# Mixer of a decoder layer, level 7: order of gate projection, output projection, gates, residual and moments

## The reference

```python
z = tanh((x + delta * mu_x) @ W_x1.T)             # delta: shifted x minus x
mus = einsum(z, W_x2) + x_bias                    # five of them: r, w, k, v, g
r, k, v, g = ((x + delta * mu) @ W.T ...)         # w: tanh(... @ A_w.T) @ B_w.T + b_w
def step(S, inp):
    kv = k_t[..., :, None] * v_t[..., None, :]
    o_t = einsum('bhk,bhkv->bhv', q_t, S + u * kv)
    return exp(w_t)[..., None] * S + kv, o_t
o = (o - mean) / sqrt(var + EPS)                  # per head
o = (o * gn_weight + gn_bias) * silu(g)
return o @ W_o.T
```

## Time and profile before

| | |
|---|---|
| median of the runs | 1555.5 us |
| profiled execution | 1543.22 us, span 1541.4 us |
| mean granted TensorE clock | 0.954 |
| PE busy | 1337.4 us, 87% of the span |
| PE weight loads (PEld) | 898.5 us, 58% |
| DVE busy | 992.6 us, 64% |
| POOL busy | 798.2 us, 52% |
| ACT busy | 576.4 us, 37% |

### The profile page before, as it was taken

The page is one execution under the profiler, slowest core; times in us unless marked ns, Lnnn a source line. Parts: engine busy times, 40 slices in busy tenths (PEclk is TensorE's granted clock), DMA queues, the critical chain, the costliest instruction groups (busy, mean ns, idle before and its releaser), DMA issues. The chain is left out here.

```text
span 1541.4 us, 31333 instructions
## 1 busy us (share of the span) xinstructions
PE 1337.4 (87%) x9914; PEld 898.5 (58%) x9915; DVE 992.6 (64%) x2041; ACT 576.4 (37%) x1420; POOL 798.2 (52%) x1138
## 2 busy tenths in 40 slices
PE   4787788778863899999999999999983999999996
PEld 2465455456552566666666666666652566666664
DVE  2687977977872378888888888888882222222221
ACT  1334233233320355555555555555541221212221
POOL 3235623633533567777777777777763222222222
PEclk9999999999976699999999999999995999999999
DMA  4995000000001554545455555555431223222231
GB/s 144 278 294 155 0 1 1 0 0 0 1 1 33 96 101 105 126 121 125 120 126 122 126 123 122 126 124 124 118 84 42 45 43 46 44 44 45 43 48 21
DMA packets 152681, 127.99 MB, mean 83 GB/s; under 512 B 41363, under 2 KB 145443, under 8 KB 152547
## 3 DMA queue, kind: packets, MB, share of 16 engines
q1 hardware_dynamic: 140242, 112.22, 29.7%
q0 software_dynamic: 12304, 14.10, 6.0%
HBM read 36.10 MB, written 44.83 MB: 53 GB/s over the span
## 5 line engine op out<-in xcount | busy, mean ns | idle before, releaser
L1365 DVE TENSOR_REDUCE neg_raw<-bank_s 100x2 f32<-100x722 f32 x256 | 229.0, 895 | 22.9 <-PE bank_s L1558 22.7
L1899 POOL DMA_INDIRECT out<-result,target x57 | 88.2, 1547 | 267.1 <-DVE result L1873 264.0
L1239 ACT ACTIVATE prob<-bank_st 120x400 f32<-120x400 f32 (+1 forms) x384 | 166.2, 514 | 152.2 <-PE bank_st L1577 152.2
L1376 DVE TENSOR_SCALAR bank_st<-bank_st 121x1200 f32<-121x1200 f32 x128 | 180.4, 1409 | 1.4 <-PE bank_st L1568 0.6
L751 PE MATMUL bank_l<-q_heads,k 128*100 128x192 f32 (+4 forms) x512 | 124.1, 383 | 63.9 <-DVE attn L565 51.0
L1884 DVE TENSOR_TENSOR hidden<-silu,ebank_v 128x512 f32<-128x512 f32 x57 | 39.2, 687 | 197.0 <-PE ebank_v L1808 197.0
L751 PEld LDWEIGHTS bank_l<-q_heads,k 128*100 128x100 f32 x512 | 81.4, 177 | 114.0 <-DVE attn L565 43.5
L399 ACT ACTIVATE q_heads<-q 32x192 f32<-32x192 f32 (+3 forms) x168 | 62.1, 369 | 226.1 <-DVE q L524 217.7
L1094 POOL TENSOR_TENSOR neg_diag<-xident_b,neg_max 100x400 bf16<-100x400 bf16 x128 | 109.1, 853 | 35.2 <-DVE neg_max L1370 34.6
L1558 PE MATMUL bank_s<-k_st,q_st 96*128 96x361 bf16 x512 | 123.2, 322 | 3.8 <-DVE neg_raw L1365 2.4
L1568 PE MATMUL bank_st<-q_st,k_st 96*128 96x100 bf16 x1536 | 112.8, 209 | 5.7 <-ACT prob L1239 0.6
(11 more groups left out here) (207 smaller groups left out, 2737.8 us busy)
## 6 DMA issues: line engine op xcount, KB each, us to landing
k_st<-k_part SPq DMA_DIRECT2D x384, 90.2 KB
slot_rows<-empty SPq DMA_DIRECT2D x9, 2967.0 KB, 28.8
q_st<-q_part SPq DMA_DIRECT2D x192, 50.0 KB
kv<-in_ctx_t SPq DMA_DIRECT2D x32, 270.8 KB
expert_w<-in_w SPq DMA_DIRECT2D x16, 512.0 KB, 4.4
rows<-slot_rows SPq DMA_DIRECT2D x57, 129.0 KB, 2.0
residual<-in_w SPq DMA_DIRECT2D x16, 256.0 KB, 4.3
residual<-in_x SPq DMA_DIRECT2D x8, 400.0 KB
```

What stands on the lines that cost most here:

```text
L1239: act.activation(prob[0:KEYS[c], t % 2, c], bank_st[0:KEYS[c], c, 0:4 * T], ACT.Exp).then_inc(exp_done, 1)
L1365: dve.tensor_reduce(neg_raw[:, h:h + 2], bank_s[0:T, :, 0:S], AX.X, ALU.max, negate=True).then_inc(max_done, 1)
L1376: dve.tensor_scalar(tile, tile, CLAMP, -CLAMP, ALU.min, ALU.max).then_inc(clipped, 1)
```

## The change

Nothing is computed otherwise. Four things change their place in the engines' programs.

- DVE: `norm_stats(g + 2)` goes from the begin of level 5 to level 7, behind the copies of that level. `front(g + 1, ..., 7)`, the two gates, goes ahead of `residual(g - 1)`, and `norm_apply(g + 2)` behind both.
- PE: in level 7 the gate projection (`front(g + 1, 7)`) goes ahead of `project_out(g - 1)`.
- POOL: `norm(g + 2)` goes behind `mix(g + 1, 4)`.
- ACT and SP keep their programs.

```diff
--- before.py
+++ after.py
@@ -315,10 +315,10 @@
                     mix(g + 1, 3)
                 if not first:
                     finish(g - 1, 1 - p, 3)
+                if more:
+                    mix(g + 1, 4)
                 if two_more(g):
                     norm(g + 2)
-                if more:
-                    mix(g + 1, 4)
             every_group(pool, body)
             head_norm(GROUPS - 1)
             for j in range(G):
@@ -611,8 +611,6 @@
                 for s in range(LEVELS):
                     if s == 0 and more:
                         front(g + 1, 1 - p, 1)
-                    if s == 5 and two_more(g):
-                        norm_stats(g + 2)
                     if s + 1 < LEVELS:
                         if s >= 1:
                             decay_q(g, p, s + 1)
@@ -630,11 +628,13 @@
                     if s == 1 and not first:
                         head_scale(g - 1)
                     if s == 7 and two_more(g):
-                        norm_apply(g + 2)
+                        norm_stats(g + 2)
+                    if more and s > 1:
+                        front(g + 1, 1 - p, s)
                     if s == 7 and not first:
                         residual(g - 1)
-                    if more and s > 1:
-                        front(g + 1, 1 - p, s)
+                    if s == 7 and two_more(g):
+                        norm_apply(g + 2)
             every_group(dve, body)
             head_stats(GROUPS - 1, 0)
             head_stats(GROUPS - 1, 1)
@@ -795,10 +795,10 @@
                     level(g, p, s)
                     if s == 6 and not first:
                         turn_out(g - 1)
+                    if more and s > 0:
+                        front(g + 1, s)
                     if s == 7 and not first:
                         project_out(g - 1)
-                    if more and s > 0:
-                        front(g + 1, s)
             every_group(pe, body)
             weigh(GROUPS - 1, (GROUPS - 1) % 2)
             turn_out(GROUPS - 1)
```

## The result

| | before | after |
|---|---|---|
| median | 1555.5 us | 1571.7 us |
| range | 1554.5 to 1556.4 (4 runs) | 1567.9 to 1574.4 (4 runs) |
| profiled execution, span | 1543.2, 1541.4 | 1570.6, 1568.7 |
| mean granted TensorE clock | 0.954 | 0.937 |
| PE busy | 1337.4 | 1363.3 |

A forecast was written before the change was run, and what follows sets the result against it. It held that PE and DVE take turns, neither full. Body 0 +0.97, bodies 1 to 5 -1.65, back branch -0.6 and body 6 +1.03 gave -0.25 us: 1555.2 from 1555.5, range 1550.0 to 1560.5.

The forecast's parts named there:

- Part 1: Moments out of level 5, bodies 0 to 5: gain of 0.81 us per body, 0.62 in body 0.
- The comparison with body 6: Body 6 has no moments in level 5: 4.30 us there against 5.11 in body 2, so 0.81 gained of 1.85.
- the rule that the prediction cites: Level 5: a two-SBUF-input DVE operation and a GpSimd operation reading SBUF exclude each other; without it, 1.85 us gained per body.
- Part 2: Level 7, bodies 1 to 5: transposes start at 207.7 instead of 206.7, `delta` comes 0.48 us later per body.
- the branch's 1.06: Loop's back branch, body 3 to 4: DVE's extra wait for `delta`; gain between 0.21 and 1.06 us, 0.6 taken.
- Part 3: The ends: body 0 loses 1.59 us at `delta`, body 6 loses 1.03, the back branch gains 0.6.
- PE gains 1.25 of idleness and gets 2.4 in its place: Ahead of the transposes in level 7: the old 1.25 us idle stretch of PE goes, a 2.4 us one comes.
- Slower, by the clock: Rival: the gap ahead of the transposes lowers TensorE's clock in bodies 1 to 5, 1.40 us each, 1562.2 us; chance 0.13.
- It decides from three bodies on: Said of the slower clock rival: falls in three or more of bodies 1 to 5 would decide the outcome.
- the 2 us gap ahead of level 6: Argument against the slower clock rival: a body's window holding this gap has a granted clock of 1.00.

The follow-up runs named there:

- e3: Kernel before, with only the moments moved from level 5 to level 7 (and `norm` behind the last mix): 1548.8 us, ratio 0.9963.
- e1: Changed kernel with four matmuls of constant weights filling PE's gap ahead of the transposes: 1551.1 us, ratio 0.9984 to the kernel before.
- e10: Changed kernel with the moments back in level 5 and the gap filled by four matmuls: 1544.3 us, ratio 1.0010 to the kernel before.
- e6: Kernel before with one more wait on PE, making the gap ahead of the transposes some 2.1 us long: ratio 1.0036.
- e7: Changed kernel with two matmuls in the gap, leaving 1.21 to 1.33 us of it in bodies 2 to 6: ratio 1.0000 to the kernel before.
- e5: Changed kernel with the moments (and `norm`) back where they were, gap not filled: ratio 1.0065 to the kernel before.
- e2: Changed kernel with `norm_apply` between the two gates instead of behind `residual`: 1543.3 us, ratio 0.9931 to the kernel before.
- e9: Changed kernel with `norm_apply` between the gates and the old order of projections, residual and gates in body 6: 1539.5 us, ratio 0.9916 to the kernel before.
- e4: Kernel before with projections swapped and gates ahead of `residual`, `norm_apply` still first in level 7, moments in level 5: 1549.0 us, ratio 0.9966.
- c1: The changed kernel unaltered, run again on another chip: ratio 1.0104 to the kernel before.
- e8: Kernel before with the longer wait on PE, the added part filled by two matmuls: ratio 1.0009 to the kernel before.
- c2: Changed kernel with the moments back in level 5, gap not filled, run again on another chip: 1551.3 us, ratio 1.0055 to the kernel before.

## Why the prediction was wrong

It said 1555.2 (1550.0 to 1560.5) and "the same"; measured was 1571.7.

*Part 1* was right: 0.81 us per body forecast, 4.30 us from `q` to `part` found, 5.7 us of gain in e3 by itself and 0.9 per body between e1 and e10. The comparison with body 6 held: of the 1.85 us about half came back, and `total` takes 0.93 us as there. That DVE waits there for POOL, by the rule that the prediction cites, is isolated by no run; and the reading that POOL has nothing else to do beside the 0.17 us of body 0 was wrong, since a small `rstd` operation of POOL (84.65, 0.29 us) ran just then.

*Part 2* was right in its order and its times: the transposes 5.81 us behind the projection's begin (5.87 forecast). `delta` follows them by 1.68 us in e1 where 1.53 was forecast. Without falls a body of the changed kernel takes 54.0 to 54.1 us (e1), and the forecast was 54.33 - 0.33 = 54.0. Still e1 is 3.2 us faster than the kernel before and not 0.25: body 4, in which the kernel before has two falls and takes 58.45 us, takes 54.13 in e1. Of these 4.3 us the forecast has 1.4 (0.33 and the branch's 1.06); the falls are the likely rest, and the sum had left them standing.

*Part 3*: body 6 lost its microsecond (`weigh` released by `residual` 4.49 us behind the output projection's begin, 4.48 forecast), and at the back branch `delta` in e1 is released by ACT 1.68 us behind the transposes as anywhere, so the whole 1.06 was gained instead of 0.6.

*What failed* is the step "PE gains 1.25 of idleness and gets 2.4 in its place", which was priced at nothing: the sum had no term for the clock. The runs showed 2.1 to 2.3 us of idleness ahead of each of bodies 2 to 6 and a fall of the clock behind it, at 3.72 us each. The rival "Slower, by the clock" was the right one; it had 0.13. Its price of 1.40 us per fall was mis-sized too. That was read in body 4, where the fall began only in level 0 and was much shorter (0.83 over 10 us, against 0.54 over 11). A fall that begins with the transposes takes in transposes, `weigh` (5.48 against 2.96) and level 0, uses up what DVE had in hand, and costs 3.72 us. With that price the rival's own sum is 1555.2 + 5 x 3.72 = 1573.8. That it comes so near to 1571.7 is in part luck: six begins fell and not five (body 0 leaves a gap of 3.29 us ahead of body 1, which the text did not work out), and the base holds the falls that the kernel before has itself. And "It decides from three bodies on" stood beside a gap that the text knew to be in all of them. Against the rival I had set the 2 us gap ahead of level 6 that passes without a fall. That argument weighed too much: e6 has the same gap with and without a fall, so that one gap passed says little of another.

The mixer as a whole ends at 509.9 us of the profile after, 493.0 before: 16.9 us, close to the 16.2 between the medians. The Trainium skill, "TensorE: Matmul & The Clock Gate", Part 1, has it that activity releases the lower clock; the trace agrees, in that matmuls of no use in the gap (e1) hold the clock at 1.00.

## What to carry to other kernels

Before an order is changed, ask for each engine where its idle time will stand afterwards, not only how much there will be: 2.2 us in one piece ahead of TensorE work cost up to 3.7 us per body, where pieces of 1.3 us brought no fall at that place in e7 and one in e3. Price a fall of the clock by the work that would run behind it at that place, not by another fall elsewhere: here one fall cost 0.6 us where DVE leads (e7), 1.7 where PE works without a break (e10), 2.1 when it began behind the transposes (e5, e6) and 3.7 when it began with them and lasted longest. And where one instruction on another engine opens such a gap, look for a hole ahead of it (here the wait between two gates) before anything is given up: with `norm_apply` there the changed order was 11 us faster than the kernel before (e2), and 13 with the old order kept in body 6 (e9).

## What was unexpected

Attention takes one of two lengths, by the chip. Its 32 first normalizations, before and after:

```profile
L1357 DVE BATCH_NORM_STATS2 xstats<-residual x32: 412/415/428, 501.3 to 1100.4; 100x6 f32<-100x256 f32 x32
```

```profile
L1357 DVE BATCH_NORM_STATS2 xstats<-residual x32: 412/415/428, 518.8 to 1127.2; 100x6 f32<-100x256 f32 x32
```

599.1 us from the first to the last before, 608.4 after, with the same code. The length goes with the session and not with the kernel: 609.7, 609.8, 610.8 and 609.6 in e1 to e4 (one chip), 608.3 to 609.2 in c1, e7, e8 and e9 (another), 599.4 and 598.4 in e5 and e6 (a third), 598.6 and 599.1 in e10 and c2 (a fourth). The kernel before, too, takes 1543.9 and 1544.0 us in the latter two sessions and 1552.7 to 1555.5 in the others. So the profile of before, 12.3 us under the median, was very likely taken on a chip of the quicker kind, and the 27.3 us between the two profiled executions are 16.9 of the change, some 9.3 of the chip, and a remainder of 1.1. Nothing in the runs tells what differs between the chips.
